# Second layer of a two-layer transformer kernel: GpSimd's expert sums dealt out tile by tile, seven heads' ranks on VectorE, and another order of one head's first steps

## What is computed

```
q5 = (x @ Wq).reshape(b, t, H, E, DH)              # H, E, DH = 8, 5, 64; x is normalised
kv = (x @ Wkv).reshape(b, t, 2, H, E, DH)
ms = _topk_mask(sigmoid(x @ Ws), 3); md = _topk_mask(sigmoid(x @ Wd), 3)
q = einsum('bthed,bthe->bhtd', q5, sd * md)        # k, v alike, with ss * ms
out = softmax(q k^T / 8) v                         # every token sees all 2048
o5 = einsum('bthd,dm->bthm', out, Wo).reshape(b, t, H, E, DIM)
y  = einsum('bthem,bthe->btm', o5, md)
```

## Time and profile before

| | us |
|---|---|
| median of 3 runs | 1756.18 |
| lowest and highest | 1745.38, 1766.88 |
| the profiled execution | 1751.98 |
| its span, first to last instruction | 1750.2 |

### The profile page before, as it was taken

The page is one execution under the profiler, slowest core; times in us unless marked ns, Lnnn a source line. Parts: engine busy times, 40 slices in busy tenths (PEclk is TensorE's granted clock), DMA queues, the critical chain, the costliest instruction groups (busy, mean ns, idle before and its releaser), DMA issues.

```text
span 1750.2 us, 27131 instructions
## 1 busy us (share of the span) xinstructions
PE 1579.0 (90%) x8404; PEld 1030.2 (59%) x8404; DVE 1224.0 (70%) x2500; ACT 942.0 (54%) x1582; POOL 843.9 (48%) x944
## 2 busy tenths in 40 slices
PE   3799999998999867798899999989989999999998
PEld 2555565565665456566566566666665665666565
DVE  4997786786787357576777676677766776766764
ACT  3446657657655612454645654655545546555652
POOL 2620000000011143878588588588587686776442
PEclk9699999999999967899999999999999999999998
DMA  2000000000000000000000000000000000000000
GB/s 61 0 1 1 1 1 1 1 1 1 1 1 1 12 12 1 1 13 1 5 9 1 12 1 1 12 1 1 12 1 1 12 1 1 1 1 1 1 7 19
DMA packets 12230, 9.39 MB, mean 5 GB/s; under 512 B 3840, under 2 KB 11584, under 8 KB 12096
## 3 DMA queue, kind: packets, MB, share of 16 engines
q1 hardware_dynamic: 12096, 7.66, 1.6%
HBM read 6.61 MB, written 1.05 MB: 4 GB/s over the span
## 4 chain that ended last, share of the span: by engine, by line
PE 67%; POOL 16%; DVE 9%; issue 4%; ACT 4%; SPq 1%; DMA 0%; DVEq 0%; ACTq 0%; POOLq 0%
PE ps L884 11%; PE ps L697 8%; PE ps L731 7%; PE ps L716 7%; PE ps L857 5%; PE ps L872 5%; POOL z L569 5%; PE ps L873 4%; POOL onm L563 4%; PE ps L664 4%; PE ps L839 2%; PE ps L895 2%; PE ps L841 2%; PE ps L840 2%; DVE mxp L1198 2%
## 5 line engine op out<-in xcount | busy, mean ns | idle before, releaser
L1077 ACT ACTIVATE pbuf<-ps 128x512 f32<-128x512 f32 x512 | 302.2, 599 | 177.1 <-PE ps L873 173.8
L973 ACT ACTIVATE pbuf<-ps 128x1024 f32<-128x1024 f32 (+3 forms) x320 | 280.3, 897 | 182.3 <-PE ps L719 92.0
L1198 DVE TENSOR_REDUCE mxp<-ps 128x1 f32<-128x512 f32 (+2 forms) x432 | 279.2, 686 | 82.3 <-PE ps L697 51.4
L1402 DVE TENSOR_TENSOR den<-den,pbuf 128x1024 f32<-128x1024 f32 x224 | 294.5, 1315 | 2.0
L1354 DVE TENSOR_TENSOR gt<-ps,gate 128x320 f32<-128x320 f32 x384 | 182.4, 485 | 122.2 <-POOL h_v L1533 65.3
L884 PE MATMUL ps<-pbuf,h_v 128*64 128x512 f32 x1024 | 248.4, 606 | 0.0
L1375 DVE CUSTOM_DVE_ANT_0 relu<-ps,relu 128x512 f32<-128x512 f32 x256 | 174.8, 686 | 99.2 <-PE ps L857 93.2
L1063 ACT ACTIVATE relu<-ps 128x512 f32<-128x512 f32 x256 | 152.1, 597 | 169.0 <-PE ps L857 130.6
L872 PE MATMUL ps<-q1T,k1T 128*128 128x512 f32 x512 | 218.4, 427 | 24.9 <-ACT q2T L1068 15.9
L697 PE MATMUL ps<-kM,qT 128*128 128x512 f32 (+3 forms) x640 | 230.2, 412 | 9.2 <-ACT kM L960 4.9
L716 PE MATMUL ps<-qT,kM 128*128 128x512 f32 (+3 forms) x640 | 199.5, 381 | 8.6 <-ACT pbuf L973 8.6
(11 more groups left out here) (227 smaller groups left out, 2738.3 us busy)
## 6 DMA issues: line engine op xcount, KB each, us to landing
wraw<-in_Wkv SPq DMA_DIRECT2D x16, 160.0 KB, 2.5
wraw<-in_Wq SPq DMA_DIRECT2D x8, 160.0 KB, 2.2
out<-x SPq DMA_DIRECT2D x4, 256.0 KB, 2.3
wqkv<-in_wqkvT SPq DMA_DIRECT2D x1, 192.0 KB, 4.1
masks<-in_masks SPq DMA_DIRECT2D x1, 128.0 KB, 4.1
dft<-in_dft SPq DMA_DIRECT2D x1, 128.0 KB, 2.2
wout<-in_Wo SPq DMA_DIRECT2D x2, 64.0 KB, 2.7
ident<-in_ident SPq DMA_DIRECT2D x1, 64.0 KB, 5.8
```

The lines of the kernel that those rows point to most:

```text
L973: nc.scalar.activation(pbuf0[:, u % NP0, :, off:CH], ps[:, b:b + 2, off:CH], ACT.Exp, scale=float(D0) ** -0.5).then_inc(s_exp, 1)
L1077: nc.scalar.activation(pbuf1[:, u % NP1, i, :], ps[:, i, :], ACT.Exp, scale=float(D1) ** -0.5).then_inc(s_exp1, 1)
L1198: v.tensor_reduce(mxp[:, i, h:h + n, b], sc.rearrange("p (h k) -> p h k", h=n), AX.X, ALU.max).then_inc(s_read0d, 1)
L1402: v.tensor_tensor(dn, dn, w, ALU.add).then_inc(s_den1, 1)
```

## The change

Three edits, in all of which the same arithmetic is done.

`by_expert` loses its loop and becomes one turn of it, and a new background step ("z", chunk, i), i from 0 to 4, calls it on POOL. Turn i multiplies tile i (i below 4) and adds tile i-1 (i above 0). The turns stand 3.6 units and then every 0.8 unit behind the chunk (every 0.35 in the last head). The wait for F's division moves from F to turn 0. POOL's instructions are the same, in number and shape.

The ranks of heads 1 to 7 go from POOL to DVE, in two parts: heads 1 to 3 at place -0.05, between head 0's last preparation and unit 0's first projection, and heads 4 to 7 at 2.65. `gate` of head 4 and up waits for the second part.

In head 0's list, the first key difference `kd[0]` comes later, behind the projection of key tile 15; `dif[0]` comes behind the values' projection of tile 1, and `dif[3]`, `mx[2]` behind the transposes of chunk 3 and `kd[1]`.

```diff
--- before.py
+++ after.py
@@ -98,12 +98,13 @@
     dif, mx = ([(kind, 0, i, p) for p in range(NC // 2) for i in range(TPC)] for kind in ("dif", "max"))
     out = [("gates",)] + k[0:4]
     out += [q[0], q[1], hik[0], q[2], q[3], lok[0], k[4], k[5], hiq[0], k[6], t[0][0], t[0][1], k[7], loq[0]]
-    out += [k[8], hik[1], k[9], k[10], t[0][2], lok[1], k[11], k[12], hik[2], k[13], t[1][0], t[1][1], kd[0]]
-    out += [k[14], lok[2], k[15], dif[0], v[0], t[2][0], t[2][1], hik[3], dif[1], mx[0], v[1], lok[3]]
-    out += [dif[2], mx[1], v[2], dif[3], mx[2], t[3][0], t[3][1], kd[1], v[3], ("ranks",), mx[3]]
+    out += [k[8], hik[1], k[9], k[10], t[0][2], lok[1], k[11], k[12], hik[2], k[13], t[1][0], t[1][1]]
+    out += [k[14], lok[2], k[15], kd[0], v[0], t[2][0], t[2][1], hik[3], v[1], dif[0], dif[1], mx[0], lok[3]]
+    out += [dif[2], mx[1], v[2], t[3][0], t[3][1], kd[1], dif[3], mx[2], v[3], mx[3]]
     out += [dif[4], dif[5], mx[4], dif[6], mx[5], dif[7], mx[6], mx[7], ("m", 0, 0), ("q2", 0, 0)]
     assert len(set(out)) == len(out)
     out = [(0.1 * (i - len(out)), step) for i, step in enumerate(out)]
+    out += [(-0.05, ("ranks", 1, 4)), (2.65, ("ranks", 4, H1))]
     at = lambda n: REST1[0] + REST1[1] * (n - TPC)
     for n in range(TPC, NT):
         out += [(at(n), q[n]), (at(n) + 0.2, v[n])]
@@ -454,6 +455,9 @@
                 after0.append((u + 0.8 * a, step))
 
         after1 = []
+        for mc in range(NC * H1 - 1):
+            u = M1 * (mc + 1) + 3.6
+            after1 += [(u + (0.35 if mc // NC == H1 - 1 else 0.8) * i, ("z", mc, i)) for i in range(TPC + 1)]
         for n in range(NT):
             u = U1 * (H1 - 1) + M1 * (n // TPC + 1) + 3
             after1 += [(u + 3.5 + n % TPC, ("zt", n)), (u + 5 + n % TPC, ("y", n))]
@@ -554,19 +558,18 @@
                 ins = eng.tensor_tensor(a[:, :, :, half:D0], a[:, :, :, half:D0], t[:, :, :, 0:half], ALU.add)
             return ins
 
-        def by_expert(queue, eng, mc):
+        def by_expert(queue, eng, mc, i):
 
             h, c = mc // NC, mc % NC
-            for i in range(TPC + 1):
-                if i < TPC:
-                    n = TPC * c + i
-                    eng.tensor_tensor(onm[:, i], on[:, i, :].unsqueeze(1).to_broadcast([P, E1, D1]),
-                                      topk[:, n, 0, h, :].unsqueeze(2).to_broadcast([P, E1, D1]),
-                                      ALU.mult).then_inc(s_onm, 1)
-                if i:
-                    n = TPC * c + i - 1
-                    queue.wait_ge(s_onm, TPC * mc + i)
-                    eng.tensor_tensor(z[:, n], z[:, n], onm[:, i - 1], ALU.add).then_inc(s_z, 1)
+            if i < TPC:
+                n = TPC * c + i
+                eng.tensor_tensor(onm[:, i], on[:, i, :].unsqueeze(1).to_broadcast([P, E1, D1]),
+                                  topk[:, n, 0, h, :].unsqueeze(2).to_broadcast([P, E1, D1]),
+                                  ALU.mult).then_inc(s_onm, 1)
+            if i:
+                n = TPC * c + i - 1
+                queue.wait_ge(s_onm, TPC * mc + i)
+                eng.tensor_tensor(z[:, n], z[:, n], onm[:, i - 1], ALU.add).then_inc(s_z, 1)
 
         block = ctx.enter_context(nc.Block())
 
@@ -1343,8 +1346,10 @@
                     dve.wait_ge(s_pconst, 3)
                     link(ranks(v, link, slice(0, 1)))
                     gates(0)
+                elif kind == "ranks":
+                    ranks(v, link, slice(*step[1:])).then_inc(s_rank, 1)
                 elif kind == "gate":
-                    dve.wait_ge(s_rank, 1)
+                    dve.wait_ge(s_rank, 1 if step[1] < 4 else 2)
                     gates(step[1])
                 elif kind == "proj":
                     _, h, n, j = step
@@ -1413,7 +1418,8 @@
                     if m == NC * H1 - 1:
                         wait_read(dve, ring1, step)
                         dve.wait_ge(s_z, TPC * m)
-                        by_expert(dve, v, m)
+                        for i in range(TPC + 1):
+                            by_expert(dve, v, m, i)
                 elif kind == "y":
                     n = step[1]
                     wait_turn(dve, ring1, step)
@@ -1500,9 +1506,6 @@
             for step in SEQ1:
                 if step[0] == "w":
                     split_weights(step[1])
-                elif step[0] == "ranks":
-                    pool.wait_ge(s_sig, 1)
-                    ranks(g_, link, slice(1, H1)).then_inc(s_rank, 1)
                 elif step in SUMS_POOL and step[3] < 2:
                     _, h, n, j = step
                     wait_read(pool, ring1, step)
@@ -1545,14 +1548,13 @@
                         pool.wait_ge(s_den1, u + 1)
                         dn = den[:, mc % 2, 0, :]
                         g_.tensor_tensor(dn, dn, den[:, mc % 2, 1, :], ALU.add).then_inc(s_den1s, 1)
-                elif step[0] == "F":
-                    mc = step[1]
-                    if mc == NC * H1 - 1:
-                        continue
-                    wait_read(pool, ring1, step)
-                    if mc:
-                        pool.wait_ge(s_z, TPC * mc)
-                    by_expert(pool, g_, mc)
+                elif step[0] == "z":
+                    _, mc, i = step
+                    if i == 0:
+                        wait_read(pool, ring1, ("F", mc))
+                        if mc:
+                            pool.wait_ge(s_z, TPC * mc)
+                    by_expert(pool, g_, mc, i)
 
 
 _INPUTS = {
```

## The result

| | before | after |
|---|---|---|
| median us | 1755.29 of 4 runs | 1688.42 of 4 runs |
| lowest, highest | 1745.38, 1766.88 | 1685.12, 1693.84 |
| span of the profiled execution | 1750.2 | 1685.8 |
| ratio of the times (95%) | 1 | 0.962 (0.9555 to 0.9684) |

The account below looks back on a forecast made before the run. PE was taken as the bound, made to wait through DVE and ACT by POOL's bursts. Savings of 49 + 8 + 3 + 1 = 61 us gave 1691 from the profiled 1751.98, 1695 beside the median; range 1674 to 1728.

Parts of the forecast that it names:

- A head, 8.1 us from 126: Heads 1 to 6: PE's waits and half clock, 9.3 us, less 1.2 for POOL being late, saved per head.
- 8.1 x 6 = 49: Saving per head multiplied over heads 1 to 6, 49 us in all.
- the 1.2 us left for a late POOL: Heads 1 to 6: deduction per head because POOL, 84% busy, will be late at places it now isn't.
- First, second and third burst: Expert sums delaying tiles in each head: PE waits of 2.5, 2.0 + 0.7 and 2.4 us would go.
- The bounds below: POOL's queue limits the projected stretch: 5.0 us saved a head, 33 in all, time 1723; rival's chance 0.19.
- Head 0's bursts, 8 us: Head 0's two bursts: 4.5 + 1 of clock and 2.5 us saved, 8 us; bounds 3 and 11.
- The ranks, -3: Moving ranks of heads 1 to 7 from POOL to DVE saves 3 us; bounds -5.3 and +4.
- 0 to 1 us on PE: Ranks' second part stops DVE 4.7 us at unit 3; PE's five banks carry about 5, costing PE 0 to 1.
- POOL's earlier start, 5.3 us: With ranks on DVE, POOL can start its first tile about 723.5, 5.3 us earlier.
- The order, -1: Head 0's new order shortens PE's 2.84 us stand at the first `dif`: -1 us; bounds -2.8 and +1.2.
- Slower, by contention: Rival: POOL turns beside busy DVE take 3.72 us instead of 2.19, +26 us, time 1782; chance 0.05.
- more than forecast: Rival: all stalls and half clock of every head go, 75 us saved, 1681 or some more; chance 0.05.

Follow-up runs that it names:

- pieces: Changed kernel with the second part of the ranks (heads 4 to 7) cut into five pieces at 2.65, 3.65, 4.65, 7.7 and 8.7: 1694.77 us, ratio 0.9665.
- 1.2 units: Changed kernel with the turns of the expert sums every 1.2 units instead of 0.8: 1687.41 us, ratio 0.9616.
- the late second part: Changed kernel with the second part of the ranks (heads 4 to 7) at place 7.7 instead of 2.65: 1690.77 us, ratio 0.963.

## Why the prediction was right, and where its terms were off

**What bounds the kernel**: right. PE's waits named DVE and ACT, and the cause was POOL's burst; with the turns together the waits come back, and spaced they go.

**A head, 8.1 us from 126**: right for the heads that it was read from. Head 1 went from 125.7 to 118.1, head 3 from 126.0 to 118.0, and in head 3 the two parts of the sum are there: PE's idle time fell by 6.3 us (9.1 to 2.8; forecast 7.6 - 1.2 = 6.4) and its busy time, by the clock, by 1.7 (116.89 to 115.17; forecast 1.7). Mis-sized was the step "8.1 x 6 = 49": I multiplied what I had read in two heads whose clock was 0.99, and heads 2, 4, 5 and 6 had 0.96 or 0.97 and took up to 128.9 us. The half clock that the bursts brought was worth 763.5 - 6 x 126 = 7.5 us more than I had, and 55.3 came for 49. The row was there: one window for each head would have shown it. That the 1.2 us left for a late POOL came out is in part luck: 0.7 of it is the wait on `sk`, which I had counted as saved and which stayed.

**First, second and third burst**: all three waits vanished as reasoned, but for that 0.7 us on `sk`, which I had counted with the second burst and which stayed, spaced or not. It wasn't the burst's. PE's new waits on `gt` are 0.4 + 0.3 us.

**The bounds below** (POOL the bound, 5.0 a head) were too careful. POOL went from 84% to 88% of the projected stretch and nothing of the gain was lost there. At 1.2 units even a larger sum of waits on POOL cost nothing to be seen.

**Head 0's bursts, 8 us**: 7.2 (z steps alone against before) or 8.0 (147.8 to 139.8, the change against everything but the z steps), in head 0 itself. Of the 7.2, 5.4 are PE's idle time (15.9 to 10.5 us) and 1.8 its busy time; the forecast had 7 and 1.

**The ranks, -3**: 2.4 up to head 1 with the new order, but not by the way forecast, so that the agreement is luck. The durations were close, 4.15 us for 4.0 and 5.1 with the gaps for 4.7, and the first sums of values started at 721.76, for 723.5. One step that failed is "0 to 1 us on PE": the banks carried 3, not 4 to 5 us, PE stood 2.19, and the clock took up to 4.3 more, a cost that this step had not been given, although half clock behind a stall had been priced in the second burst. The other is that POOL's earlier start, 5.3 us, would come back as idle time of PE: in head 0 that is 10.3 us with the ranks on POOL, 10.0 with them on DVE and 10.0 with pieces. What changed is the clock, which in the same move with the old order went the other way, 2.4 us against it. The pieces' 6.1 us against the ranks on POOL (42.8 + 141.5 for 42.0 + 136.2) are mostly clock too, 5.0 us of PE's busy time. What POOL's earlier start is worth by itself no run tells.

**The order, -1**: 1.4 us in the stretch ahead of head 0 with the ranks on DVE, 1.7 with them on POOL (43.7 to 42.0); the stretch of before and of the z steps alone, which are the same there, differ by 0.8. The first wait fell from 2.84 to 1.52 us. Its effect in head 0 itself stays open.

**Slower, by contention**: the mechanism is real, and it was priced right by the means, 2.31 us a turn with 3.2 as the point where it decides. The hindered shares that I read from the means, a fifth and a third, were 27 and 47 of 124.

**The sum** was 61, the profile says 64.4, and the 3.4 between them are several misses that partly cancel: +6.3 in heads 1 to 6; -2.5 ahead of and in head 0, where 12 were forecast (8 + 3 + 1) and 9.5 came; -0.6 in the last head, which I had put at nothing; +0.3 in the part in front. The last head's 0.6 is not the turns' spacing of 0.35 there: seven other kernels with the same spacing take 118.3 to 118.4 us for it, before 118.4, the turns together in the earlier heads 120.9, and the pieces 116.6, at clocks of 0.93 in after, 0.94 in before and 0.97 with pieces. The 9.5 us step by step, from profile to profile: 6.4 with the z steps alone, 0.7 more with the order, 2.4 more with the ranks; in the other sequence the ranks cost 2.4 and the order then gives 5.5, so only the first of these steps stands by itself. The 7 us between 1695 and the median are less than the same program moved by: measured again it had a median of 1697.5. Nor can the total tell the forecast from the rival of more than forecast, whose 1681 lies inside the forecast's own 1674 to 1714; the heads do, since not all of their stalls went.

## What to carry to other kernels

An engine that is half idle over the run can still cost the bottleneck time, where its work comes in one piece in front of something short that others wait for; deal the piece out at about the spacing at which the short things come. Judge the result by the longest single wait against the buffers that stand behind it, not by the sum of the waits, and look at PE's busy time for the same instructions beside its idle time: in head 0 here kernels that differed by 2 to 5 us had the same idle time within 0.3 us, and the clock made the difference. Read each repetition of a loop (here: one window a head) before multiplying what one shows.

## What the runs showed of the hardware

- Stalls of PE of 2.19, 1.41 and 0.35 us came with a granted clock of 0.80 and 0.69 in two windows of 10 us, that is partly the 1.2 GHz level; stalls of 2.02, 0.74 and 1.24 us, the same 4 us of idle time, came with 1.00. With the turns 1.2 apart the same steps ran at 1.00 and then 0.83.
- An instruction of POOL that starts while DVE adds two SBUF tiles of 1024 f32 elements waits for the end of that addition: 34 of 124 multiplications took 1631 to 1782 ns and the others 709 to 905, none between. Without these additions none took over 978.
- DVE is held by POOL too: these additions took 1.21 to 1.22 us where no POOL instruction was running when they started (37 of 224), and up to 1.89 where one was. In the kernel with the late second part the ranks' instructions of 384 elements took 1.10 and 1.11 us beside POOL's `wl` (three in 3.61 us), where the same shape takes 0.56 in after.
- The part of the kernel that no edit touched varied by 9 us between two profiles of the same program, at clocks of 0.75 and 0.66 from 600 to 676 us; the heads behind it repeated within 0.3 us.
